# Cross-attention on one core: the mask turned by DMA transposes instead of TensorE, with another prologue and another tail

## The reference

```python
Q = _split_heads(query @ Wq.T + bq, B, LQ)
K = _split_heads(key @ Wk.T + bk, B, LK)
V = _split_heads(value @ Wv.T + bv, B, LK)
scores = jnp.einsum('bhqd,bhkd->bhqk', Q, K) / np.sqrt(HD)
scores = jnp.where(mask[:, None, :, :] == 0, jnp.float32(-1000000000.0), scores)
attn = jax.nn.softmax(scores, axis=-1)
ctx = jnp.einsum('bhqk,bhkd->bhqd', attn, V)
out = ctx.transpose(0, 2, 1, 3).reshape(B, LQ, H) @ Wo.T + bo
x = out + query          # then a layer norm over the last axis
```

## Time and profile before

| | |
|---|---|
| median of 3 runs | 1708.9 us (1706.65 to 1711.57) |
| the profiled execution's own time | 1710.62 us |
| its span, first to last instruction | 1708.8 us |
| mean granted TensorE clock | 0.979 |
| PE busy | 1651.7 us, 97% |
| ACT, POOL, DVE busy | 79%, 76%, 68% |
| DMA queue of SP | 66.5% of the 16 engines' span |

### The profile page before, as it was taken

How to read it: one execution, slowest core, us unless ns; L and a number is a source line. 1 busy time by engine, 2 the same in 40 slices (tenths; PEclk the granted TensorE clock), 3 DMA queues, 4 the chain that set the end, 5 groups by cost and what they waited for, 6 DMA issues and landing times.

```text
span 1708.8 us, 24796 instructions
## 1 busy us (share of the span) xinstructions
PE 1651.7 (97%) x7728; PEld 983.5 (58%) x7728; DVE 1153.9 (68%) x2835; ACT 1343.3 (79%) x1538; POOL 1290.9 (76%) x835
## 2 busy tenths in 40 slices
PE   4789999999999999999999999999999999999987
PEld 3555656565665656566565656656565665656532
DVE  6556676767667676766767776676766667677653
ACT  2278788887988888798888878888887878879774
POOL 4065787977878797787878778788878878877775
PEclk8889999999999999999999999999999999999988
DMA  9758567675866766676776767677577667757601
GB/s 355 211 138 237 175 200 200 201 216 160 242 182 197 204 204 188 198 225 183 214 198 184 211 201 210 191 203 216 173 213 210 201 177 211 217 158 192 168 9 68
DMA packets 181058, 330.65 MB, mean 193 GB/s; under 512 B 37440, under 2 KB 37440, under 8 KB 180928
## 3 DMA queue, kind: packets, MB, share of 16 engines
q1 hardware_dynamic: 180928, 329.08, 66.5%
HBM read 239.87 MB, written 89.13 MB: 193 GB/s over the span
## 4 chain that ended last, share of the span: by engine, by line
PE 90%; DMA 3%; DVE 3%; POOL 1%; ACT 1%; issue 1%; SPq 0%; POOLq 0%; DVEq 0%; ACTq 0%
PE proj_bank L928 44%; PE ctx_bank L857 14%; PE ring L826 13%; PE exp_banks L841 13%; PE ring L877 3%; DMA stack_scratch<-qk_lo 2%; PE ring L886 1%; PE exp_banks L964 1%; POOL total L428 1%; DMA w_scratch<-q_stack 1%; DVE qk_lo L683 0%; DVE ring L655 0%; ACT probs L536 0%; POOL total L436 0%; ACT qk_hi L556 0%
## 5 line engine op out<-in xcount | busy, mean ns | idle before, releaser
L655 DVE CUSTOM_DVE_ANT_0 ring<-ring,bias 128x512 f32<-128x512 f32 x1024 | 691.0, 710 | 345.3 <-PE ring L826 345.1
L536 ACT ACTIVATE probs<-exp_banks 128x1024 f32<-128x1024 f32 x512 | 523.9, 1023 | 244.7 <-PE exp_banks L841 244.1
L510 ACT CAST exp_banks<-biasT 128x1024 f32<-128x1024 bf16 x512 | 520.7, 1017 | 23.6 <-ACT probs L536 0.7
L841 PE MATMUL exp_banks<-q_stack,k_stack 98*128 98x512 f32 x1024 | 377.2, 450 | 3.5 <-ACT exp_banks L510 3.4
L826 PE MATMUL ring<-k_stack,q_stack 96*128 96x512 f32 x1024 | 331.0, 402 | 6.0 <-DVE maxes L655 3.3
L436 POOL TENSOR_TENSOR total<-total,probs 128x1024 f32<-128x1024 f32 x126 | 297.4, 2382 | 9.3 <-POOL total L428 0.4
L428 POOL TENSOR_TENSOR total<-total,probs 128x2048 f32<-128x2048 f32 x63 | 289.8, 4600 | 10.5 <-ACT probs L536 4.0
L428 POOL TENSOR_TENSOR total<-probs 128x2048 f32<-128x2048 f32 x63 | 289.9, 4602 | 0.1
L857 PE MATMUL ctx_bank<-probs,v 128*32 128x512 f32 x2048 | 278.2, 616 | 0.7 <-DVE ctxT L716 0.7
L443 POOL CAST max_parts<-maxes 128x16 fp32r<-128x16 f32 x64 | 12.6, 198 | 336.0 <-DVE maxes L655 336.0
L841 PEld LDWEIGHTS exp_banks<-q_stack,k_stack 98*128 98x128 f32 x1024 | 195.3, 192 | 110.5 <-issue 67.4
(11 more groups left out here) (78 smaller groups left out, 1879.0 us busy)
## 6 DMA issues: line engine op xcount, KB each, us to landing
w_tile<-w_scratch SPq DMA_DIRECT2D x126, 512.0 KB, 4.6
k_stack<-stack_scratch SPq DMA_DIRECT2D x192, 256.0 KB, 5.4
q_stack<-stack_scratch SPq DMA_DIRECT2D x192, 256.0 KB, 7.1
stack_scratch<-qk_hi SPq DMA_DIRECT2D x128, 256.0 KB, 2.2
stack_scratch<-qk_lo SPq DMA_DIRECT2D x128, 256.0 KB, 2.6
raw<-cT_dram SPq DMA_DIRECT2D x64, 256.0 KB, 4.9
raw<-xT_dram SPq DMA_DIRECT2D x64, 256.0 KB, 4.9
raw<-mask_dram SPq DMA_DIRECT2D x64, 256.0 KB, 4.3
```

What stands on the lines that cost most here:

```text
L510: nc.scalar.copy(exp_banks[:, 2 - 2 * wave:4 - 2 * wave, :], biasT[:, kc:kc + 1, :].to_broadcast([P, 2, L])).then_inc(seeded, 1)
L536: nc.scalar.activation(probs[:, u % PS, 2 - 2 * wave:4 - 2 * wave, :], exp_banks[:, 2 - 2 * wave:4 - 2 * wave, :], ACT.Exp).then_inc(exps, 1)
L655: nc.vector.tensor_tensor_reduce(out=ring[:, n % 2], in0=ring[:, n % 2], in1=bias[:, c], scale=1.0, scalar=LOWEST, op0=ALU.subtract, op1=A ...
L841: mm = nc.tensor.matmul(exp_banks[:, h], k_stack[0:3 * D + 2, at, kc * P:(kc + 1) * P], q_stack[0:3 * D + 2, at, :], start=False, stop=Tru ...
```

## The change

Four things change.

1. **The mask.** `turn_mask` moves from PE to SP: 4 DMA transposes of 128 x 128 bf16 from `bias` straight into `biasT`, in units 12, 13, 14 and 15. `copy_mask` on DVE and the identity are gone; the minus sign is now the scale of ACT's `seed`. The mask no longer takes turns in `ring`. ACT waits for the transposes' semaphore.
2. **Weight tiles made on chip.** The first four tiles of Q and K take their weights from DVE (`make_weights`) instead of the first two; the big splits for `w_scratch` go to ACT (high parts) and POOL (low parts), from unit -10.
3. **Another order ahead of the loop.** The stores to `w_scratch`, Wo and the constants are issued after the first stacks; the mask of the first sequence is loaded earlier; the first tiles alternate between `proj_bank` and `ctx_bank`; PE runs idle products (`keep_awake`) in units -12 to -7.
4. **Last tiles in free banks.** The first three of four products of two last output tiles move into units 253 and 254, into `proj_bank` and the free bank of `ring`.

```diff
-    MASKS = {13: 0, 14: 1, 15: 2, 1: 3}
+    MASKS = {12: 0, 13: 1, 14: 2, 15: 3}
...
     def mask(self, y):
-        s, kc = (y + 3) // UPS, self.MASKS.get(y % UPS)
+        s, kc = (y + 4) // UPS, self.MASKS.get(y % UPS)
...
+            def turn_mask(s, kc):
+                sp.wait_ge(bias_ready, (s + 1) * NC)
+                if s >= 1:
+                    sp.wait_ge(seeded, 2 * (s * UPS - NC + kc) + 2)
+                for c in range(NC):
+                    sp.dma_start_transpose(biasT[:, kc, c * P:(c + 1) * P],
+                                           bias[:, c, kc * P:(kc + 1) * P]).then_inc(
+                                               mask_turned[kc], FULL)
...
             for y in range(START, END):
-                if y == -13:
+                if y == -8:
+                    load_weight(WoT, wo[:, :, :], wo_loaded)
+                    for dst, src in ((bv_s, bv), (bo_all, bo), (g_all, ln_g), (b_all, ln_b)):
+                        sp.dma_start(dst[:, :], src).then_inc(consts_loaded, FULL)
                     scratch(0, (ctxT[:, 0:NG], q_stack[:, 2 * HG:3 * HG].bitcast(FP32)), wk_split,
                             wk_scratch)
-                if y == -10:
-                    scratch(1, (total[:, :, :], rows[:, :, :]), wq_split, wq_scratch)
-                if y == -9:
-                    stack("K", 0)
...
+                    if PLAN.qk[tile] < 2:
+                        stack(tile[0], 0)
+                if y == -7:
+                    scratch(1, (total[:, :, :], rows[:, :, :]), wq_split, wq_scratch)
+                tile = PLAN.tile(y + (1 if y < -4 else 2))
+                if tile and tile[0] in "QK":
                     load_weights(tile)
...
+                if PLAN.mask(y):
+                    turn_mask(*PLAN.mask(y)[1:])
...
                 if u % UPS < NC:
-                    act.wait_ge(ring_free, PLAN.ring["M", s, kc] + 1)
+                    act.wait_ge(mask_turned[kc], FULL * NC * (s + 1))
...
-                nc.scalar.copy(exp_banks[:, 2 - 2 * wave:4 - 2 * wave, :],
-                               biasT[:, kc:kc + 1, :].to_broadcast([P, 2, L])).then_inc(seeded, 1)
+                nc.scalar.activation(exp_banks[:, 2 - 2 * wave:4 - 2 * wave, :],
+                                     biasT[:, kc:kc + 1, :].to_broadcast([P, 2, L]),
+                                     ACT.Copy, scale=-1.0).then_inc(seeded, 1)
...
-            def copy_mask(s, kc):
-                n = PLAN.ring["M", s, kc]
-                dve.wait_ge(ring_filled, n + 1)
-                if s >= 1:
-                    dve.wait_ge(seeded, 2 * (s * UPS - NC + kc) + 2)
-                nc.vector.tensor_copy(biasT[:, kc], ring[:, n % 2]).then_inc(ring_free, 1)
...
+            def last_output(n, t):
+                if n == 0 and t == 0:
+                    pe.wait_ge(normed, LAST)
+                    pe.wait_ge(o_out, PLAN.o["O", NB - 2, NC - 1] + 1)
+                if n == 1 and t == 0:
+                    pe.wait_ge(ring_free, PLAN.ring["S", LAST - 1] + 1)
+                if n >= 2 and t == 0:
+                    pe.wait_ge(exps, 2 * UNITS)
+                if n == 0 and t == NK - 1:
+                    pe.wait_ge(normed, GROUPS)
+                mm = nc.tensor.matmul(last_bank(n), ctxT[:, (GROUPS - NG + t) % CS,
+                                                         n * P:(n + 1) * P],
+                                      wo[:, t], start=t == 0, stop=t == NK - 1)
...
+                if y - UNITS + 3 in (0, 1):
+                    for t in range(NK - 1):
+                        last_output(y - UNITS + 3, t)
```

More of the change, by code:

```diff
@@ L38 @@
 SS, PS, CS, RAW, WS = 3, 3, 5, 7, 2
+MADE = 4
 KEPT = 4
@@ L75, in __init__ @@
                 kinds[tile] = len(kinds)
+        self.second_bank = [tile for tile, n in self.no.items() if n % 2 and n < 8]
         for n in range(NC):
@@ L80, in __init__ @@
             for item in (self.score(y, 0), self.score(y, 1), self.score(y, 2), self.score(y, 3),
-                         self.mask(y), self.sums(y)):
+                         self.sums(y)):
                 if item:
@@ L116, in before @@
     def before(self, tile):
-        return self.at[max(y for y in self.at if y < self.unit[tile])]
+        same = [y for t, y in self.unit.items() if y < self.unit[tile]
+                and (t in self.second_bank) == (tile in self.second_bank)]
+        return self.at[max(same)] if same else None
 PLAN = Plan()
@@ L210, in xattn_program @@
         tail_done, tail_biased = sem("tail_done"), sem("tail_biased")
+        mask_turned = [sem(f"mask_turned{n}") for n in range(NC)]
         mask_scaled, o_biased = sem("mask_scaled"), sem("o_biased")
@@ L683, in finish_tile @@
                     nc.vector.scalar_tensor_tensor(
-                        out=qk_lo[:, :], in0=proj_bank[:, 0],
+                        out=qk_lo[:, :], in0=bank(tile),
                         scalar=(bq_s if kind == "Q" else bk_s)[:, n:n + 1],
@@ L745, in _ @@
                 tile = PLAN.tile(y - 1)
-                ring_wanted = PLAN.sums(y) or PLAN.mask(y)
+                ring_wanted = PLAN.sums(y)
                 if tile and tile[0] == "O":
@@ L894, in projection @@
                 if half == 0:
-                    if PLAN.no[tile]:
-                        b = PLAN.before(tile)
+                    b = PLAN.before(tile)
+                    if b:
                         if b[0] in "QK":
@@ L924, in projection @@
                         parts += [(wh, hi[:, t]), (wl, hi[:, t]), (wh, lo[:, t])]
+                if seq == 0 and n == 0 and kind in "QK":
+                    parts = [p for m, p in enumerate(parts) if m % 3 < 2] + parts[2::3]
                 middle = len(parts) // 2 - len(parts) // 12
@@ L940, in _ @@
                 score(y, 1)
-                if PLAN.tile(y - 1):
+                if y >= 0 and PLAN.tile(y - 1):
                     projection(PLAN.tile(y - 1), 1)
```

171 lines of the change are left out of this document (87 added, 84 removed).

## The result

The changed kernel takes 1838.5 us (median of 4 runs, 1833.2 to 1840.2); the kernel before took 1710.2 beside it. The ratio is 1.0745, with a 95% interval of 1.0719 to 1.0771: 7.5% slower, where 1678 was forecast.

A forecast was written before the change was run, and what follows sets the result against it. The prediction took PE to bound the kernel, with 90% of the span. Mask 15, transposes on SP 0, prologue 16 and tail 1 gave 1710.6 - 15 - 0 - 16 - 1 = 1678.6, said as 1678 us, range 1664 to 1692.

The forecast's parts named there:

- h: Time one DMA transpose holds SP's queue: bounded by 0.42 and 1.4 us, taken at the lower bound, so cost 0.
- The sign: The whole change turns slower once stalls eat the 32 us of gains, 2.1 us a sequence, from h = 0.97 on.
- the upper part: The case of a hold of 1 us and more on SP's queue: 1710 to 1870 us, chance 0.30.
- 12h - 9.5: PE's wait in us for late stacks, at unit 18's first plain score, in each of 15 sequences, with a middle credit.
- The margin: Time to spare between the stacks' landing and unit 18's first plain score: 5.5 us, plus 3.0 of SP idle time.
- a credit: 1.6 us more to spare on SP if the maxima's store takes its median 1.4 us instead of 3.
- The rival: Each transpose holds SP, stacks come late, PE waits in unit 18: 1710 to 1870 us, chance 0.30 for 1 us and more.
- the worst case: Stalls at a hold of 1.4 us, each followed by lower clock losing 5.5 us of work, in every sequence: 1870 us.
- The mask in the loop: 60 groups of four mask products leave PE at 0.25 us each: 15 us gained, between 12 and 20.
- The prologue: Third K tile at 48.6 against 64.49: 16 us gained, 8 if next inputs' loads and transposes of units -4 to -1 lengthen it.
- the lower end: For the hold: 0.42 us, an ordinary DMA issue in a row of three. For the time ahead of the loop: 8 us gained.
- The tail: Six of the last sixteen products move into units 253 and 254: 1 us gained, from a loss of 3 to a gain of 3.

The follow-up runs named there:

- experiment 8: The changed kernel with its narrow transposes in units 12, 13, 14 and 0, so eight stand ahead of the stacks instead of twelve: 1780.2 us, ratio 1.0364.
- experiment 7: The kernel before with only the mask moved to DMA, one 128 x 512 transpose a unit, prologue and tail as before: 1702.7 us, ratio 0.9923.
- experiment 1: The changed kernel with the mask back on TensorE in units 13, 14, 15 and 17, all else as changed: 1703.3 us, ratio 0.9956.
- experiment 4: The changed kernel with one 128 x 512 transpose a unit in place of four of 128 x 128: 1694.4 us, ratio 0.9898.
- experiment 10: The changed kernel with one 128 x 512 transpose a unit, run once more: 1693.1 us, ratio 0.9902.
- experiment 9: The kernel with one wide transpose a unit, with all transposes left out and so no mask in the shifted scores: 1694.0 us, ratio 0.9902.

## Why the prediction was wrong

**The step that failed** is the size of h, the hold of a transpose on SP's queue: "I take the lower bound: the row nearest in kind is another SP queue instruction that only describes a transfer". The bounds were 0.42 and 1.4 us; it measured 1.23. That both stand in one queue does not make a transpose like a copy. The sign turned at 0.97, near the middle of the bounds, and no row spoke for the lower end; a chance of 0.30 for the upper part was too little.

**The rest of that step held.** The place (the first plain score of unit 18) and the form of the sum were right: 12h - 9.5 gives 5.3 us a sequence at 1.23, and 6.1 were measured. Two of its numbers were off. The margin was 0.9 us too wide by the misreading of the landing (experiment 8). The store of the maxima did return faster, 1.76 us in place of 3.0, a credit of 1.2 and not of 1.6. With both, 12h - 8.8 gives 6.0, and the sign turns at some 0.9. That it comes so close is in part luck: in the sequence above the ordinary issues and their gaps took back 1.4 us of what the idle time gave, and the stacks landed 1.3 us sooner (8.0 us behind their first issue, 9.3 before). The first sequence has its stall too (PE L853 at 99.37), so there are 16 and not 15. The rival named the lower clock behind a stall as well, and priced the worst case at 5.5 us; it is 1.7 to 3.0 us behind each. In all 98 us of stalls and 45 of lower clock stand against gains of some 16. One sum is off by a little: from the ends of its terms the fastest time is 1666, not 1664; nothing hangs on it.

The Trainium skill ("VectorE: DVE Perf Modes", section The three transpose paths) has 1309 ns for a 128 x 128 transpose by DMA, by which the rival gave 6.2 us a sequence; the trace agrees for this size (1.23 us of queue, 6.1 us). The page gives no other size, and does not say whether its time is that of the queue or of the transfer; here a 128 x 512 transpose held the queue for 1.22 us as well.

**The mask in the loop, 15 us** (12 to 20). The groups did go, but 9 to 13 us came of them. The page and the waits of experiment 7, beside 1651.7 us busy of a span of 1708.8 before:

```profile
PE 1633.7 (96%) x7472; PEld 968.3 (57%) x7472; DVE 1116.1 (66%) x2771; ACT 1344.0 (79%) x1538; POOL 1288.2 (76%) x835
```

```profile
PE proj_bank L924 <- DVE qk_lo L698: 8.3, 10, 2.0
```

PE's busy time fell by 18.0 us, and its idle time rose by 7.5 (from 57.1 to 64.6). Between experiments 1 and 4 the two are 15.7 and 9.8. Waits of PE for `qk_lo` from 182 to 1600 us rose from 1.2 to 8.3 with the mask alone, and from 2.9 (experiment 1) to 6.6 and 10.0 (experiments 10 and 4): 4 to 7 us given back there. Whether the gain is nearer 9 or 13 stays open. The term was over-sized because it took PE's own time as gain and did not ask which engine PE would next catch up with; DVE at 70% and ACT at 83% busy looked like cover, but one product waits for one tile of theirs.

**The prologue, 16 us** (8 to 20). Measured 9.4 with the mask on PE (unit 0 at 76.33), inside the ends. First scores came at 33.6 (31 forecast), the third K tile at 53.0 (48.6): 11.5 us of gain there. The rest of the way, left at 21.2 us, took 23.4 in experiment 1 (52.95 to 76.33) and 27.0 in the change. In the changed kernel unit 0 came only at 80.0, because eight transposes of units -4 and -3 hold SP for 10 us ahead of the maxima's loads (64.32 to 75.4 us); with the wide ones it came at 76.45. The prediction had that as a reason for the lower end.

**The tail, 1 us** (-3 to 3). From the sums of the last group to the end it took 40.4 us before (1668.37 to 1708.8), 41.5 in the change (1794.91 to 1836.4) and 41.2 in experiment 1: nothing gained, 1 us lost, inside the ends. The cause of that microsecond was not looked for.

With h at 0.31 us a narrow transpose, which is what the wide ones amount to (1.23 over four), the sum of the prediction would have stood with these two terms smaller: 1710.6 - 9 - 0 - 9 + 1 is 1693.6, and 1694.4 was measured. This is a check that the terms add up, not a forecast, for the nines and the one are measured ones.

## What to carry to other kernels

A queue is an engine: before moving work from a busy engine to a DMA queue, multiply the number of instructions by the hold of one, and look for who waits behind them. Where the hold is unknown and the sign hangs on it, one wide instruction in place of many narrow ones removes the question. A time for the removed work is a gain only up to the next engine that must keep pace, so look for the one instruction that the freed engine will meet first.

## What the hardware did that was not expected

- A DMA transpose of bf16 held SP's queue for 1.23 us, against 0.42 for a copy's issue (1.31 for three), and the same 1.22 us for 128 x 128 as for 128 x 512.
- The transposes move in small packets: those under 512 B went from 37440 to 78368 over the kernel. With wide transposes there are 72224, and the wide ones cost nothing that could be measured (experiment 9). So it is not the packets that cost most of the 128 us; that narrow ones, with 18% more added packets, cost nothing by their traffic is not shown.
- A stall of 5.7 us on PE at full clock was followed by a window of 13 us at 0.78. Over the 16 stalls, 97.8 us, the windows behind them lost 38 us: such a stall costs about four tenths of its length again.
